# Cross-attention scores on half of the array's rows: two heads side by side, four heads in a unit's first slot

## The reference, cut to what matters

```python
q = x @ Wq.T + bq; k = context @ Wk.T + bk; v = context @ Wv.T + bv
q = q.reshape(B, NQ, 16, 16)          # 16 heads of 16; k and v likewise
attn = jnp.einsum('bihd,bjhd->bhij', q, k) * SCALE
attn = jax.nn.softmax(attn, axis=-1)  # 112 queries x 375 keys
out = jnp.einsum('bhij,bjhd->bihd', attn, v)
```

## Time and profile before

| what | value |
|---|---|
| median of 3 runs | 3142.16 us (3135.05 to 3143.45) |
| the profiled execution | 3136.99 us, its span 3135.2 us |
| PE busy with matmuls | 2746.9 us, 88% of the span |
| PE's weight loads | 2247.6 us, 72% |
| DVE, ACT, POOL busy | 1498.8, 1113.3 and 638.5 us (48%, 36%, 20%) |

### The profile page before, as it was taken

How to read it: one execution, slowest core, us unless ns; L and a number is a source line. 1 busy time by engine, 2 the same in 40 slices (tenths; PEclk the granted TensorE clock), 3 DMA queues, 4 the chain that set the end, 5 groups by cost and what they waited for, 6 DMA issues and landing times. The chain is left out here.

```text
span 3135.2 us, 58175 instructions
## 1 busy us (share of the span) xinstructions
PE 2746.9 (88%) x19352; PEld 2247.6 (72%) x19352; DVE 1498.8 (48%) x3187; ACT 1113.3 (36%) x2348; POOL 638.5 (20%) x660
## 2 busy tenths in 40 slices
PE   4999994996999998499999969899789999849992
PEld 2767672674888887488888857666578888848882
DVE  3455556335767664500000036555567777553334
ACT  1222235332555553033333324332145555402220
POOL 0000000003333331022222200000143333104542
PEclk8899996997999997599999989999889999859996
DMA  5000001786777772255655668600168888415666
GB/s 135 23 23 22 22 22 31 245 283 164 191 189 190 188 191 66 67 176 177 207 178 194 202 195 296 224 1 1 42 157 210 204 204 205 111 35 183 206 212 195
DMA packets 284132, 459.92 MB, mean 147 GB/s; under 512 B 73234, under 2 KB 211956, under 8 KB 284004
## 3 DMA queue, kind: packets, MB, share of 16 engines
q1 hardware_dynamic: 267236, 408.97, 46.0%
q0 software_dynamic: 16768, 49.30, 4.8%
HBM read 339.13 MB, written 119.02 MB: 146 GB/s over the span
## 5 line engine op out<-in xcount | busy, mean ns | idle before, releaser
L1389 ACT ACTIVATE x_probT<-banks 125x448 f32<-125x448 f32 x768 | 418.0, 544 | 402.3 <-PE banks L1292 392.6
L1495 DVE TENSOR_REDUCE x_neg_max<-banks 112x2 f32<-112x750 f32 x512 | 455.8, 931 | 97.7 <-PE banks L1276 97.7
L2000 PE MATMUL banks<-f_xT,f_w 128*128 128x256 f32 (+1 forms) x1680 | 368.7, 376 | 24.5 <-DMA f_b<-in_L_ffn_b 9.7
L2000 PEld LDWEIGHTS banks<-f_xT,f_w 128*128 128x128 f32 x1680 | 310.0, 196 | 76.6 <-issue 11.6
L1433 POOL TENSOR_TENSOR x_diag<-ident,x_neg_max 112x448 fp32r<-112x448 f32 x256 | 240.8, 941 | 575.4 <-DVE x_neg_max L1495 553.5
L2012 PE MATMUL banks<-f_w,f_hT 128*128 128x256 f32 x1584 | 354.3, 380 | 0.0
L1290 PE MATMUL banks<-x_diag,x_ones 112*125 112x448 f32 x768 | 324.5, 423 | 10.5 <-POOL x_diag L1433 9.8
L2012 PEld LDWEIGHTS banks<-f_w,f_hT 128*128 128x128 f32 x1584 | 296.2, 191 | 37.5
L1292 PEld LDWEIGHTS banks<-x_qP,x_kP 128*125 128x125 f32 x1536 | 291.3, 190 | 14.9
L1292 PE MATMUL banks<-x_qP,x_kP 128*125 128x224 f32 x1536 | 291.5, 271 | 0.0
L1276 PE MATMUL banks<-x_kP,x_qP 128*112 128x376 f32 x1024 | 264.5, 341 | 10.4 <-DMA x_qP<-q_halves 9.6
(11 more groups left out here) (321 smaller groups left out, 4096.7 us busy)
## 6 DMA issues: line engine op xcount, KB each, us to landing
x_kP<-k_halves SPq DMA_DIRECT2D x512, 188.0 KB, 3.6
f_w<-in_L_ffn_w SPq DMA_DIRECT2D x70, 1024.0 KB
f_w<-in_L_ffn_w SPq DMA_DIRECT2D x70, 512.0 KB
x_qP<-q_halves SPq DMA_DIRECT2D x512, 56.0 KB, 3.2
x_v<-v_rows SPq DMA_DIRECT2D x64, 408.0 KB, 3.2
k_halves<-p_halves SPq DMA_DIRECT2D x32, 752.0 KB, 3.6
k_halves<-f_d_halves SPq DMA_DIRECT2D x32, 752.0 KB, 4.0
q_halves<-x_q_halves SPq DMA_DIRECT2D x64, 224.0 KB, 2.3
```

Of the source, the lines that this page charges most:

```text
L1389: act.activation(probT[:, u % 2, c].rearrange("k h t -> k (h t)"), ST[i % 2][0:KB, 0:HU * T], ACT.Exp).then_inc(exp_done, 1)
L1495: dve.tensor_reduce(mx[:, u % RING, 2 * pair:2 * pair + 2], psum[0:T, 2 * pair:2 * pair + 2, 0:NKV], AX_X, ALU.max, negate=True).then_inc( ...
L2000: last = pe.matmul(bank[1 + f % 3][:, 0:width], w1[:, r, k, f * P:(f + 1) * P], xT[:, r, k, 0:width], start=(k == 0), stop=(k == KD - 1))
```

## The change

`score(g, u, pair)` becomes `scores(g, u)`, which issues both pairs of a unit. It is called in slot 0 only, and slot 1 is left with its `exponent` and the jobs. `values` stays in slot 2. Each score matmul now reads only the 64 partitions of its own head, of `qP` and of `kP`: the first head of a pair on rows 0 to 63 of the array, the second on rows 64 to 127. The number of matmuls (four in a unit, each with one weight load), their columns (112 of weights, 376 moving) and their output banks stay. The wait of pair 1 on `max_done` keeps its count but is now reached in slot 0. Nothing of DVE, ACT, POOL or SP is changed.

```diff
+    ROWS = (slice(0, HALF), slice(HALF, P))
...
-                def score(g, u, pair):
+                def scores(g, u):
...
-                    n = 2 * u + pair
-                    if pair == 0 and q % 2 == 0:
+                    if q % 2 == 0:
                         pe.wait_ge(k_loaded[q // 2][r], g * (32 * GROUP) + 64 * (s // 2 + 1))
-                    if pair == 0 and q == 0:
+                    if q == 0:
                         pe.wait_ge(q_loaded[s], g * 128 + 128)
-                    pe.wait_ge(max_done, ONE + since(g, 2 * NU, n - 1))
-                    for k in range(2):
-                        last = pe.matmul(bank[2 * pair + k][0:T, 0:NKV + 1], qP[:, s, k, 2 * q + pair, :],
-                                         kP[:, r, 2 * q + pair, :], start=True, stop=True)
-                    last.then_inc(s_ps, 1)
+                    for pair in range(2):
+                        pe.wait_ge(max_done, ONE + since(g, 2 * NU, 2 * u + pair - 1))
+                        for k in range(2):
+                            last = pe.matmul(bank[2 * pair + k][0:T, 0:NKV + 1], qP[ROWS[k], s, k, 2 * q + pair, :],
+                                             kP[ROWS[k], r, 2 * q + pair, :], start=True, stop=True)
+                        last.then_inc(s_ps, 1)
...
-                        if c < 2 and (u + AHEAD < NU or not last):
-                            score(g, u + AHEAD, c)
+                        if c == 0 and (u + AHEAD < NU or not last):
+                            scores(g, u + AHEAD)
```

More of the change, by code:

```diff
@@ L1369, in _ @@
                 for u in range(AHEAD):
-                    for pair in range(2):
-                        score(0, u, pair)
+                    scores(0, u)
                 all_groups(pe, group)
```

## The result

The changed kernel takes 3150.52 us (median of 19 runs), the one before 3140.74 (19 runs). The ratio is 1.0033 with a 95% interval of 1.0026 to 1.0040: slower by a third of a percent, about 10 us. The forecast was 3151, +0.28%. The profiled execution took 3151.36 us, its span is 3149.6 us, 14.4 us more than the span of before. The runs of the changed kernel scatter over 14 us, those of before over 11.

A forecast was written before the change was run, and what follows sets the result against it. PE was taken to bound the kernel, busy throughout both cross-attention middles. 374 - 335 - 4 = +35 ns a unit over 252 units gave +8.8 us on 3142.16: 3151 us, +0.28%; own range 3146 to 3159, whole range 3142 to 3181.

The forecast's parts named there:

- What bounds: Middles of both cross-attention stages: PE busy for the whole window, so its time from unit start to unit start counts.
- Part 1: Score matmuls: two heads side by side turn four streams into two and a 7 ns step, gaining 335 ns a unit.
- The rival of serial halves: Score matmuls: the two row halves don't run together; 370 ns a unit, +93 us, 3235; chance 14%.
- serial loads: Score weight loads of the two halves go one after the other; 142 ns a unit, +36 us, 3178; chance 8%.
- the quicker stream: Score matmuls: a 64-row stream takes less time than a full one; +7 ns a unit, +2 us, 3144; chance 21%.
- Part 2: Around the scores: one more array shape change there and back, 89 + 89 + 96 + 100 = 374 ns in each unit.
- the first score's weights: First score matmul after the shape change: its weights aren't in yet, costing 89 ns a unit.
- The rival of a hidden trip: Shape change around the scores: next weights load while the last stream drains; 85 us less, 3057; chance 4%.
- One small term: Slot 1 without scores has no shape to switch: about 4 ns less a unit.
- Part 3: Waits: pair 1's in slot 0 bounded at 0 to 3 us, none taken; ACT's exponential and copy covered.
- The sum: Whole kernel: 374 - 335 - 4 = +35 ns a unit, over 252 units +8.8 us.

The follow-up runs named there:

- both on one half: Changed kernel with both heads of a pair on rows 0 to 63, the second head's products left out of its maxima: 3244.63 us, ratio 1.0327.
- Two trips a unit: Each head on its own 64 rows, but one pair in slot 0 and one in slot 1 as in the kernel before: 3239.67 us, ratio 1.0310.
- the order alone: Changed kernel with both pairs in slot 0, but each score matmul over all 128 rows: 3139.47 us, ratio 0.9991 to the kernel before.
- by two: Kernel before, with the values of two units computed together in every second unit: 3108.11 us, ratio 0.9900.
- by four: Kernel before, with the values of all four units of a sequence computed together in the next sequence's first unit: 3150.60 us, ratio 1.0035.

## Why the prediction was right

**What bounds.** Right: PE is busy in every window of the middles, before and after, and its matmuls wait for no other engine there. Its weight loads do, 12.3 us for ScalarE in layer 1's middle, as they did before (12.4 us), with PE busy all the same.

**Part 1, the overlap.** Right, and the one thing no row of before could show. The two of a pair start 4 ns apart (7 taken). With both on one half the burst is 0.35 us longer (0.335 taken). The rival of serial halves (14%) falls by this, serial loads (8%) by the weight loads of a pair, which start 3 ns apart, and the quicker stream (21%) by its starts of 172 ns. (The price of serial loads has a slip: four loads 98 ns apart put the last 294 ns behind the first, not 285, which makes 3180 and not 3178.) The Trainium skill, "TensorE: Matmul & The Clock Gate", section Measured speedup vs the span model, gives about 4 ns for each tile; the rows agree.

**Part 2, the trip.** Right within 6 ns a term: in 201 to 202 ns (199 taken), the first score's weights 260 - 171 = 89 (89), out 261 (267), line 1291 306 (306). The trip's price, read from self-attention and from `values`, carries over to a trip between other shapes. Two trips a unit cost +97 us, none with the same order -0.1%. The rival of a hidden trip (4%) falls. One small term had the wrong sign: slot 1, left without scores, should have become 4 ns shorter, and became 9 ns longer in units without a job (110 ns into the next line 1291 against 108, and 211 for that line against 204). Why was not tried.

**Part 3, the waits.** Right: the order alone costs nothing, and no wait of PE for DVE stands in the middle windows.

**The sum.** 35 ns a unit was forecast. Units without a job show 45, the steady mean over all is 32, which is +8.0 us for 248 units against the forecast's +8.8 for 252. The forecast said nothing of the stages' starts, another 6 us in either profile of the changed kernel against the one before (5 against the order alone, whose start in layer 1 is longer). Steady part and starts make 12 to 14 us by the traces; the medians give +9.8, and +11.0 when the changed kernel ran again. So the mechanism is right and the closeness of the total is partly luck: a term of 5 to 6 us is missing from the sum, and the medians came out 2 to 4 us below what the traces add up to. With the starts the forecast would have been 3153 to 3157 (3140.74 + 12, or 3142.16 + 8.8 + 6). Where the rest goes in a typical run stays open.

## What to carry to other kernels

The two halves of rows and the four column tiles of this kernel overlap nearly fully, but a change of the array's shape has a price of its own, 0.31 to 0.37 us there and back for operands of this size: 0.09 us of gap on each side, and weights that come late on both. Count the trips before the streams. At 0.37 us a trip and 0.17 us a stream of 376 columns, an estimate from these numbers is that overlap pays from the third stream saved on, which no run here tried. Saving trips of an existing kernel may be worth more than making another one pay (1.0% here by the medians, 0.7% by the traces). Such an edit moves work between slots, and the cover of the engines beside (ScalarE's two buffers, DVE's queue order) sets how far it can go: by two it won, by four it lost everything.

## What the runs showed of the hardware that was not expected

PE's granted clock rose later behind a pause when the first bursts were 64-row matmuls: from 1.2 to 2.4 GHz 9.8 to 10.7 us after the first score at eleven of twelve starts (7.5 at the other), 6.0 to 8.5 us at ten starts with full rows. It is not the idle time between the bursts: with 64 rows and without overlap PE was as busy (5.55 of the first 6 us) as with 128, and the rise was still late, 9.8 and 10.4 us against 7.0 and 8.5 (two starts each). What it is in the 64-row matmuls that holds the clock down stays open. The two starts together took 5 to 6 us longer with them.

A wait of PE costs more than its length where it also keeps the next weights from being loaded ahead: 0.04 us late became 0.13.
